# The last stage of a state-space mixer on one core: x products of the next step ahead of the output products, squares added on GpSimd, later weights issued by SyncE

## What is computed

```python
z  = x @ W_in[:, :512]
xs = x @ W_in[:, 512:1024]
y = SSD_SCALE * ys + D_param * xs
g = y * silu(z)
y = g * rsqrt(mean(g * g, axis=-1) + EPS) * norm_w
mixed = y @ W_out
x = layernorm(x + mixed)
```

## Time and profile before

| | us |
|---|---|
| median of 3 timed runs | 3166.25 (3165.69 to 3168.21) |
| profiled execution, its own time | 3143.08 |
| its span | 3141.3 |
| PE busy | 2333.7 (74% of the span) |
| DVE busy | 1964.0 (63%) |
| ACT busy | 1555.3 (50%) |
| POOL busy | 1455.4 (46%) |
| mixer's end, first transfer issued to the next stage's first one | 1828.33 to 2147.63 |

### The profile page before, as it was taken

How to read it: one execution, slowest core, us unless ns; L and a number is a source line. 1 busy time by engine, 2 the same in 40 slices (tenths; PEclk the granted TensorE clock), 3 DMA queues, 4 the chain that set the end, 5 groups by cost and what they waited for, 6 DMA issues and landing times. The chain is left out here.

```text
span 3141.3 us, 63603 instructions
## 1 busy us (share of the span) xinstructions
PE 2333.7 (74%) x19953; PEld 1695.6 (54%) x19954; DVE 1964.0 (63%) x5279; ACT 1555.3 (50%) x3098; POOL 1455.4 (46%) x2255
## 2 busy tenths in 40 slices
PE   7883777777777777777777738887858884776887
PEld 4552554555555554555545527776634443555887
DVE  3444777778877787777877823334632225775777
ACT  3446777777777777777777601113521111222222
POOL 2225666666666666666666610002411113442444
PEclk8775787788877888777888769988879997888999
DMA  4556555565555655555556463233422222331111
GB/s 130 166 163 161 134 140 132 134 153 134 144 137 130 147 140 145 140 124 142 140 145 146 114 210 97 87 96 107 151 81 68 69 67 87 115 117 48 40 50 34
DMA packets 303158, 374.50 MB, mean 119 GB/s; under 512 B 54116, under 2 KB 242855, under 8 KB 302439
## 3 DMA queue, kind: packets, MB, share of 16 engines
q1 hardware_dynamic: 286358, 331.96, 40.4%
q0 software_dynamic: 9872, 27.28, 2.6%
q10 hardware_dynamic: 6688, 12.23, 1.2%
HBM read 151.03 MB, written 86.05 MB: 75 GB/s over the span
## 5 line engine op out<-in xcount | busy, mean ns | idle before, releaser
L610 POOL TENSOR_TENSOR p_CR<-p_pc 128x256 f32<-128x256 f32 x512 | 374.1, 731 | 447.3 <-DVE p_pc L938 427.2
L951 DVE TENSOR_TENSOR p_M<-p_ps_sc,p_D 128x512 f32<-128x512 f32 x512 | 328.8, 684 | 300.5 <-PE p_ps_sc L693 300.4
L653 PE MATMUL p_ps_x<-p_low,p_eye 64*128 64x256 bf16 x1024 | 121.7, 323 | 410.1 <-ACT p_BT L836 362.9
L830 ACT ACTIVATE p_D<-p_ps_x 128x512 f32<-128x512 f32 x512 | 302.1, 592 | 195.5 <-PE p_ps_x L659 194.8
L616 POOL TENSOR_TENSOR p_BR<-p_pb 128x256 f32<-128x256 f32 x512 | 373.3, 729 | 25.6
L693 PE MATMUL p_ps_sc<-p_CR,p_BR 64*128 64x128 f32 x4096 | 368.8, 331 | 13.1 <-POOL p_BR L616 7.6
L693 PEld LDWEIGHTS p_ps_sc<-p_CR,p_BR 64*128 64x128 f32 x4096 | 314.7, 231 | 83.3 <-issue 50.2
L708 PE MATMUL p_ps_y<-p_M,p_uexp 128*32 128x128 f32 x4096 | 336.6, 318 | 5.4 <-POOL p_uexp L593 4.1
L653 PEld LDWEIGHTS p_ps_x<-p_low,p_eye 64*128 64x128 bf16 x1024 | 33.8, 99 | 481.1 <-ACT p_BT L836 362.6
L708 PEld LDWEIGHTS p_ps_y<-p_M,p_uexp 128*32 128x32 f32 x4096 | 241.8, 126 | 80.5 <-issue 64.1
L938 DVE SCALAR_TENSOR_TENSOR p_pc<-p_ps_c,p_beta,p_cs 128x256 f32<-128x256 f32 x512 | 243.6, 476 | 41.3 <-DMA p_sn<-p_tr_s 32.0
(11 more groups left out here) (276 smaller groups left out, 5453.8 us busy)
## 6 DMA issues: line engine op xcount, KB each, us to landing
p_cs<-p_tr_c SPq DMA_DIRECT2D x512, 128.0 KB, 2.4
p_sn<-p_tr_s SPq DMA_DIRECT2D x512, 128.0 KB, 2.4
p_phib<-scratch_phi SPq DMA_DIRECT2D x256, 128.0 KB, 3.1
p_x<-scratch_rt SPq DMA_DIRECT2D x72, 128.0 KB, 2.0
scratch_ro<-p_o POOLq DMA_DIRECT2D x72, 128.0 KB, 2.0
p_xT<-in_xT SPq DMA_DIRECT2D x64, 128.0 KB, 3.0
scratch_u<-p_u SPq DMA_DIRECT2D x16, 512.0 KB, 3.8
scratch_wu<-p_wu SPq DMA_DIRECT2D x16, 512.0 KB, 5.0
```

Of the source, the lines that this page charges most:

```text
L610: e.tensor_tensor(CR[:, p, g, :], pc[:, g % 2, 0, :], pc[:, g % 2, 1, :], ALU.add).then_inc(S["rotC"], 1)
L653: e.matmul(bank[half][:, :].rearrange("p (n l) -> p n l", l=L)[:, :, 64 * turn:64 * turn + 64], eye[r, turn, :], repeat(low[r, :], 4), sta ...
L830: e.activation(D[:, n, :], x_ps[i % 2][:, :], ACT.Exp).then_inc(S["x_ok"], 1)
L951: e.tensor_tensor(M[:, m_slot(p, n), :], sc_ps[n % 2][:, :], D[:, n, :], ALU.mult).then_inc(S["m_ok"], 1)
```

## The change

In `finish_mixer`:

- PE computes the xs products of step t+1 (`of_x`) between the z products and the output products of step t. xs of step 0 stands ahead of the loop. The output products wait for `g`, no longer for the squares. The transposes of step t-1 come after the output products, and the sums of squares after them, 2 matmuls in place of 8.
- POOL adds the four blocks of squares in two additions (`halves`, 128x512, and `total`, 128x256) ahead of its two powers.
- DVE computes `mix` of step t+1 after `g` of step t.
- ACT squares before it copies the transposes, and issues no transfers.
- SP issues the transfers of `load_ahead`, which has become a generator: three after each step's stores, in steps 0 to 9. The steps of SP are unrolled. The load's waits are unchanged.
- The last two steps of PE and DVE are unrolled too.

```diff
@@ load_ahead @@
     e.dma_start(K["w1"][:, :, :], I["sw1"].rearrange("(k p) n -> p k n", p=P)).then_inc(got, 16)
+    yield
     e.dma_start(K["w3"][:, :, :], I["sw3"].rearrange("(k p) n -> p k n", p=P)).then_inc(got, 16)
+    yield
...
@@ finish_mixer @@
+        halves, total = sb("halves", [P, 2, CT]), sb("total", [P, CT])
...
-            stream(e, load, store)
+            ahead = load_ahead(e, I, W)
+            load(0, 0)
+            load(1, 1)
+            for t in range(NC):
+                if t + 2 < NC:
+                    load(t + 2, t % 2)
+                store(t, t % 2)
+                for _ in range(3):
+                    next(ahead, None)
...
         @block.gpsimd
             def step(t, p):
+                at_least(e, S["g2_ok"], t, 2, 2)
+                e.tensor_tensor(halves[:, :, :], g2[:, 0:2, :], g2[:, 2:4, :], ALU.add).then_inc(S["half_ok"], 1)
+                at_least(e, S["half_ok"], t, 1, 1)
+                at_least(e, S["q_mm"], t, 1, 0)
+                e.tensor_tensor(total[:, :], halves[:, 0, :], halves[:, 1, :], ALU.add).then_inc(S["sum_ok"], 1)
                 at_least(e, S["ms_ok"], t, 1, 1)
...
         @block.tensor
-            def step(t, p):
+            def of_x(t, p):
                 at_least(e, S["x_in"][p], t - p, 32, 64)
                 at_least(e, S["mix_ok"], t, 2, 0)
...
                 m.then_inc(S["xs_mm"], 1)
+
+            def step(t, p):
                 at_least(e, S["silu_ok"], t, 2, 0)
...
                 m.then_inc(S["z_mm"], 1)
-                if not (isinstance(t, int) and t == 0):
-                    turn(t - 1, 1 - p)
-                at_least(e, S["g2_ok"], t, 2, 2)
+                if not (isinstance(t, int) and t == NC - 1):
+                    of_x(t + 1, 1 - p)
+                at_least(e, S["g_ok"], t, 2, 2)
                 at_least(e, S["xr_ok"], t, 2, 0)
...
-                for b in range(BATCH):
-                    for n in range(NB):
-                        m = e.matmul(q_ps[:, b:b + 1], g2[:, n, b * L:(b + 1) * L], ones[:, :], start=(n == 0), stop=(n == NB - 1))
                 m.then_inc(S["o_mm"], 1)
-            two_step_loop(e, step, NC)
+                if not (isinstance(t, int) and t == 0):
+                    turn(t - 1, 1 - p)
+                at_least(e, S["sum_ok"], t, 1, 1)
+                at_least(e, S["ms_ok"], t, 1, 0)
+                for b in range(BATCH):
+                    m = e.matmul(q_ps[:, b:b + 1], total[:, b * L:(b + 1) * L], ones[:, :], start=True, stop=True)
+                m.then_inc(S["q_mm"], 1)
+            of_x(0, 0)
+            two_step_loop(e, step, NC, 2, 2)
...
         @block.scalar
-            load_ahead(e, I, W)
...
-                if not (isinstance(t, int) and t == 0):
-                    copy_turned(t - 1, 1 - p)
-                at_least(e, S["o_mm"], t, 1, 0)
+                at_least(e, S["sum_ok"], t, 1, 0)
...
+                if not (isinstance(t, int) and t == 0):
+                    copy_turned(t - 1, 1 - p)
...
         @block.vector
-            def step(t, p):
+            def mixed(t, p):
                 at_least(e, S["x_in"][p], t - p, 32, 64)
...
+            def step(t, p):
                 at_least(e, S["mix_ok"], t, 2, 2)
...
-                at_least(e, S["o_mm"], t, 1, 1)
+                if not (isinstance(t, int) and t == NC - 1):
+                    mixed(t + 1, 1 - p)
+                at_least(e, S["q_mm"], t, 1, 1)
                 at_least(e, S["rms_ok"], t, 1, 0)
                 e.tensor_scalar(ms[:, :], q_ps[:, 0:BATCH], 1.0 / DI, EPS_RMS, ALU.mult, ALU.add).then_inc(S["ms_ok"], 1)
+                at_least(e, S["o_mm"], t, 1, 1)
```

More of the change, by code:

```diff
@@ L1117, in load_ahead @@
         e.dma_start(K[dst][:, :, :], I[src].rearrange("(k p) n -> p k n", p=P)).then_inc(got, 16)
+        yield
     e.dma_start(K["bq"][:, :], I["b_q"]).then_inc(got, 16)
+    yield
     e.dma_start(K["bk"][:, :], on_all_partitions(I["b_k"])).then_inc(got, 16)
+    yield
     e.dma_start(K["bv"][:, :], on_all_partitions(I["b_v"])).then_inc(got, 16)
+    yield
     e.dma_start(K["lw"][:, :], I["ln_w"]).then_inc(got, 16)
+    yield
     e.dma_start(K["lb"][:, :], I["ln_b"]).then_inc(got, 16)
+    yield
     e.dma_start(K["ident"][:, :], I["c_ident"]).then_inc(got, 16)
+    yield
     K, got = W["k5"], W["k5_in"]
     e.dma_start(K["raw"][:, :, :], I["gate_w"].rearrange("(k p) n -> p k n", p=P)).then_inc(got, 16)
+    yield
     e.dma_start(K["rawu"][:, :, :], I["up_w"].rearrange("(k p) n -> p k n", p=P)).then_inc(got, 16)
+    yield
     e.dma_start(K["rawd"][:, :, :], I["down_w"].rearrange("(k p) n -> p k n", p=P)).then_inc(got, 16)
+    yield
     e.dma_start(K["gs"][:, :], I["gate_scale"]).then_inc(got, 16)
+    yield
     e.dma_start(K["us"][:, :], I["up_scale"]).then_inc(got, 16)
+    yield
     e.dma_start(K["ds"][:, :], on_all_partitions(I["down_scale"])).then_inc(got, 16)
+    yield
     e.dma_start(K["wo"][:, :, :], I["w_o"].rearrange("(k p) n -> p k n", p=P)).then_inc(got, 16)
+    yield
     e.dma_start(K["bo"][:, :], on_all_partitions(I["b_out"])).then_inc(got, 16)
+    yield
 def finish_mixer(nc, held, I, W):
     with ExitStack() as ctx:
-        F = Phase(nc, ctx, held, "p2", "const_in prep fold xs_mm z_mm silu_ok mix_ok g_ok g2_ok o_mm ms_ok rms_ok xr_ok tr_mm xt_ok "
+        F = Phase(nc, ctx, held, "p2", "const_in prep fold xs_mm z_mm silu_ok mix_ok g_ok g2_ok half_ok sum_ok q_mm o_mm ms_ok rms_ok xr_ok tr_mm xt_ok "
                   + " ".join(norm_names()), "x_in stored")
@@ L1241, in step @@
                                      start=(n == 0), stop=(n == NB - 1))
+                m.then_inc(S["o_mm"], 1)
+                if not (isinstance(t, int) and t == 0):
+                    turn(t - 1, 1 - p)
+                at_least(e, S["sum_ok"], t, 1, 1)
+                at_least(e, S["ms_ok"], t, 1, 0)
                 for b in range(BATCH):
-                    for n in range(NB):
-                        m = e.matmul(q_ps[:, b:b + 1], g2[:, n, b * L:(b + 1) * L], ones[:, :], start=(n == 0), stop=(n == NB - 1))
-                m.then_inc(S["o_mm"], 1)
-            two_step_loop(e, step, NC)
+                    m = e.matmul(q_ps[:, b:b + 1], total[:, b * L:(b + 1) * L], ones[:, :], start=True, stop=True)
+                m.then_inc(S["q_mm"], 1)
+            of_x(0, 0)
+            two_step_loop(e, step, NC, 2, 2)
             turn(NC - 1, 1)
@@ L1308, in step @@
                 norm_vector(e, S, N, t, xr, x1[:, p, :, :], free)
-            two_step_loop(e, step, NC)
+            mixed(0, 0)
+            two_step_loop(e, step, NC, 2, 2)
 def stream(e, load, store):
```

## The result

The change made the kernel slower: 3181.33 us median (3174.08 to 3189.07, 7 runs) against 3166.25 (3160.05 to 3168.53, 7 runs), a ratio of 1.0049 with the 95% interval 1.0034 to 1.0065, so 11 to 21 us. The profiled execution has a span of 3179.6 us, 38 us more than the one of before. Not all of that belongs to the change: its mixer's end begins 14.3 us later, behind stages whose code is the same. The stage's own length, from its first transfer to the next stage's first one, went from 319.3 to 338.7 us, 19.4 more.

A forecast was written before the change was run, and what follows sets the result against it. PE's chain bounds the kernel's steady step; the change puts the load's wait on it. -25.7 (start) - 5.4 (first step) + 7.3 (loop) + 24.3 (weights) = +0.5 us, so 3166.7, no change; range 3148 to 3185.

The forecast's parts named there:

- the weights stand in the new cycle at full length: Slower rival: the weights' term is over 30 us or the period over 18.1; 3173 to 3185, taken as 3178, chance 0.31.
- The wait that moves onto the path: Mixer's end: PE's xs(t+2) waits for a load issued only after xr(t), closing a cycle through xr, load, xs and o.
- The period: One turn of the xr, load, xs, o cycle: 17.6 us, 0.7 more than before; bounds 16.9 and 18.4.
- The loop without weights: From xr(0) to xr(15): 14 periods of 17.6 plus a last step of 12.3, 258.7 us, a loss of 7.3.
- The start: Stage's start: without ACT's 30 transfers PE begins at 1840, not 1865.73, a gain of 25.7 us.
- The first step: From PE's first xs to the end of xr(0): 17.9 us instead of 23.35, a gain of 5.4.
- The later weights: Weights in SP's queue right ahead of the loads delay them: 24.3 us including 2 us of issue; bounds 15 and 38.
- The store and issue ahead of the load: SP's x1T store and three weight issues delay the load's issue to 17.9 from 17.75: 0.2 us a step, 2 in all.
- Nothing for POOL's additions and the shorter q: POOL's two additions and fewer square-sum products in each step cost nothing, since the wait for the load covers them.
- the clock does not fall: Faster rival: PE's clock stays high in the idle time, xs takes 3.35 us, 24.5 us less, 3142; chance 0.07.
- Loads and weights overlap better: Faster rival: landing of 4.0 us, period 17.1, and weights at 425 GB/s, 17 us: 3152; chance 0.18.
- The change does what it says: Full-gain rival: the load is not on PE's path, steps take 11.2 us, 90 us less, some 3077; chance 0.03.

The follow-up runs named there:

- weights at the start: The change, but ACT again issues all 30 later weight transfers ahead of its first step: 3161.81 us, ratio 0.9989 to the kernel before.
- the small ones alone: The change, but ACT issues the seven largest later weights at the stage's start and SP keeps the other 23: 3178.61 us, ratio 1.0046.
- the weights on ACT's queue: The change, but ACT instead of SP issues the later weights, three at the end of each of its steps: 3165.22 us, ratio 0.9998.
- the wait was filled: The change with ACT issuing all later weights before its first step, plus 9 unread PE products between z and xs: 3140.87 us.
- the load split: The change, but xT and y no longer wait for xr; x gets its own transfer, semaphore and wait: 3051.88 us, ratio 0.9652.
- the old order: The kernel before, with only the later weights moved to SP, three behind each step's stores: 3131.36 us, ratio 0.9894.
- the split load with the weights on the other queue: The change with xT and y freed from xr, x loaded separately, and ACT issuing later weights three a step: 3052.0 us, ratio 0.965.

## Why the prediction was right, and where it was wrong

The range held the result, 3181.3 in 3148 to 3185, but the likeliest case, no change at 3166.7, did not come. What came is the rival on the slower side, "the weights stand in the new cycle at full length", priced at 3178 with a chance of 0.31; its own condition, a term of the weights over 30 us, is met with 40.5. The range held with some luck: the stage alone grew by 19.4 us, which would be 3185.7, just beyond it, and the timed medians differ by 15.1 only.

- **The wait that moves onto the path**: right, and shown. The profile has 15 waits for `y`; with that wait taken from xT and y all steps but two are near 11.25 us.
- **The period**: 17.6 forecast, 17.67 measured where no weights are in the way (weights at the start), 17.14 in the best steps of the change. xs at the low clock was taken as 5.1; it took 4.8 to 6.3, 5.2 in the mean. The landing was taken as 4.6 with what PE needs to notice it; it took 4.0 to 5.0, 4.3 in the mean.
- **The loop without weights**: +7.3 forecast. With the weights at the start xr(0) to xr(15) is 257.97 us against 251.4, so +6.6. That the two agree so well is luck in part: 14 steps took 247.45 and not 246.4, and the last one 10.52 and not 12.3, since o ran at the high clock in it; in the change it took 12.19.
- **The start**: -25.7 forecast, -24.8 measured. **The first step**: -5.4 forecast, -4.6 measured.
- **The later weights**: this is the term that failed, 24.3 forecast and 40.5 measured in the 14 steps (42.2 up to xr(15), with the last step's o at the low clock), beyond even the upper bound of 38. Against a step of 17.7 the four steps behind large transfers lost 12.6, 9.9, 5.3 and 2.8 us where 9.5, 5.6, 5.0 and 1.4 were summed, 9.1 short in total. The six steps behind small ones lost 10.9 where 2.8 stood for them and the issues; the experiment with the small ones alone gives 10.2 in its 14 steps. "The rest nothing" was the worst guess: 16 KB in three transfers (`gate`, `expert_bias`, `iota`) made a step of 18.4 us, 1.3 above the quiet ones of 17.14.
- **The store and issue ahead of the load**: 0.2 us a step, 2 in all, forecast; `y` was issued later by 6.1 us in all, 2.8 of it in the one step behind the 2016 KB. In the steps behind small weights it is 0.3 to 0.5 us. The larger part there is the landing of `y`, 5.0 to 6.3 us where the quiet step has 4.15, and in four of the six xs takes 0.7 to 1.3 us longer at the low clock. Why the landing grows by 0.8 to 2.2 us behind so few bytes is open; whether each transfer holds the queue by itself or the many short rows do was not tried.
- **Nothing for POOL's additions and the shorter q**: right. Even at 11.25 us a step o never waits outside the last step, where it waits for `g` behind the norm as forecast, 2.9 us.

The forecast weighed a rule of the Trainium skill ("DMA: Bandwidth & Descriptors", "Queues, rings and completion order"): a DMA engine takes turns between its queue rows packet by packet. That the load would then take about twice its own time, and the term be 12 us, was an assumption of mine, for the page does not say that the turns are equal in bytes. With the weights on ACT's queue the load did not get half of the engines' time: 13.3 us for `xT` on either. So the assumption fails, and the rule is not refuted by it; that the turns are unequal because the rows are, is my reading and was not measured by itself. The same page's "Issuing engines are not separate DMA queues" says that issuing from several engines saves only the issue time. For the two largest transfers the run comes near that (28.4 and 26.0 us against 30.3 and 27.6), for the small ones it does not: there `y` also landed earlier, after 4.1 to 5.4 us against 5.0 to 6.3.

The other rivals: "the clock does not fall" was wrong, it fell in every step, and its price of 24.5 us was close: 23.5 less in the stage when the wait was filled. In the 14 steps it is 29.2 (218.27 against 247.45); 5.6 of that went back in the start and in the first and last steps, where the filling covers no such wait. "Loads and weights overlap better" was wrong for the weights; quiet steps came near its 17.1. "The change does what it says" would have needed the load free of `xr`. With the load split, and SP's order to go with it, that case was made: 3077 was its price, 3052 is measured. The 3077 still held the 24.3 us of the weights, which the split load hides but for two steps, and that is about the difference of 25.

## What to carry to other kernels

When work is moved ahead on one engine, look for the input that it now needs a step earlier, and follow that input's own release: a double buffer whose free signal comes from the step's end turns a hidden load into a cycle. Transfers that are free while the loads have 9 us to spare cost their time once the load is on the path, and the large ones did so whichever queue they were on. So the same move took 28.6 us off the stage in the old order and added 16.5 in the new one. Split a load by who frees its buffers, and cut large background transfers into pieces no longer than the slack (205.8 us of stage in place of 215.9; the timed runs do not show this part).

## What the runs showed of the hardware

- A small transfer ahead of a load has a price that its bytes do not tell: 23 transfers, 2.1 MB in all, cost 10.2 us in a chain of 14 waiting loads, 8.6 of it as later landings.
- 4032 KB of long rows on another queue delayed a 128 KB load as much as on the same queue (13.3 us to landing both times). In the split load with the weights on the other queue, 2016 KB issued 4.6 us after a load of 512 KB landed 4.8 us ahead of it, the load took 22.5 us to land (12.4 with all on one queue), and SP's issue of a 256 KB store took 8.86 us.
- Idle time of 4.3 to 5.3 us on PE ahead of 16 weight loads cost 1.5 to 3.0 us of low clock on them (3.32 filled; 4.8 to 6.3 unfilled). Work that nobody reads paid for itself, 23.5 us in the stage.
